# A transformer block on one core: values of two head groups projected at once, the second group's kept in DRAM

## The reference

```python
# 1. token mixer: a state space kernel with 64 poles per channel
K = jnp.einsum('chn,hnl->chl', Cm, jnp.exp(dtA[:, :, None] * jnp.arange(512)))
h = 2 * K.real
# 2. attention on layernorm(h): 16 query heads, 4 key/value heads of width 128, rotary
q = q * cos + _rotate_half(q) * sin
k = k * cos + _rotate_half(k) * sin
k = jnp.repeat(k, 4, axis=1); v = jnp.repeat(v, 4, axis=1)
probs = softmax(q @ k.T / sqrt(128) + bias)        # causal
h = h + (probs @ v) @ w_o
# 3. gated feed-forward on layernorm(h): the best of 8 gates picks a rank 8 update
h = h + _L0_ffn_ref(_layernorm(h, axis=-1), ...)
```

## Time and profile before

| | us |
|---|---|
| median of three runs | 817.11 (816.69 to 817.26) |
| profiled execution | 815.06, span of its records 813.3 |
| TensorE busy | 747.9 |
| VectorE, ScalarE, GpSimd busy | 569.0, 455.8, 445.2 |
| a step of group 1 | 19.94 |
| a loop step of group 3 | 24.5 to 24.7 |
| from the scores of the last step to the end | 43 |

### The profile page before, as it was taken

The page is one execution under the profiler, slowest core; times in us unless marked ns, Lnnn a source line. Parts: engine busy times, 40 slices in busy tenths (PEclk is TensorE's granted clock), DMA queues, the critical chain, the costliest instruction groups (busy, mean ns, idle before and its releaser), DMA issues.

```text
span 813.3 us, 19702 instructions
## 1 busy us (share of the span) xinstructions
PE 747.9 (92%) x6970; PEld 678.4 (83%) x6970; DVE 569.0 (70%) x1600; ACT 455.8 (56%) x1250; POOL 445.2 (55%) x660
## 2 busy tenths in 40 slices
PE   0366778999999999999999999999999999999997
PEld 0166667899999999999999999999999999988974
DVE  7999758787766666665566655665665777788777
ACT  6734426666665656555575665555756556455442
POOL 1497836754444747444456474444656655665632
PEclk9999999999999999999999999999999999999999
DMA  9023360100010102000001020000010000000002
GB/s 213 1 60 69 81 233 27 39 1 0 0 40 2 53 1 79 0 0 0 0 1 52 2 79 0 0 0 0 14 40 1 2 1 27 26 26 0 26 1 104
DMA packets 30503, 26.47 MB, mean 33 GB/s; under 512 B 22446, under 2 KB 22830, under 8 KB 30198
## 3 DMA queue, kind: packets, MB, share of 16 engines
q1 hardware_dynamic: 30310, 25.77, 11.2%
q10 hardware_dynamic: 144, 0.07, 0.0%
HBM read 17.44 MB, written 8.39 MB: 32 GB/s over the span
## 4 chain that ended last, share of the span: by engine, by line
PE 77%; DVE 8%; POOL 7%; ACT 4%; issue 3%; DMA 1%; DVEq 0%; SPq 0%; POOLq 0%; ACTq 0%
PE bank_quad L1324 17%; PE bank_quad L1326 16%; PE bank_quad L1325 16%; PE bank_pair L1326 4%; PE bank_pair L1324 4%; PE bank_pair L1325 4%; POOL w_lo L433 2%; PE bank_quad L1336 2%; PE bank_quad L1425 2%; PE bank L1501 1%; PE bank_pair L1491 1%; PE bank L1505 1%; PE bank_pair L1501 1%; DVE bank_pair L974 1%; POOL kq_lo L511 1%
## 5 line engine op out<-in xcount | busy, mean ns | idle before, releaser
L1324 PE MATMUL bank_quad<-xt_hi,w_hi 128*128 (+1 forms) x768 | 217.0, 282 | 1.4 <-POOL w_lo L433 0.8
L1326 PE MATMUL bank_quad<-xt_lo,w_hi 128*128 (+1 forms) x768 | 214.7, 280 | 0.0
L1325 PE MATMUL bank_quad<-xt_hi,w_lo 128*128 (+1 forms) x768 | 214.5, 279 | 0.0
L1062 DVE TENSOR_TENSOR kq<-bank_quad,cst 128x512 f32<-128x512 f32 (+1 forms) x96 | 57.8, 602 | 134.8 <-ACT swap L725 101.2
L506 POOL TENSOR_TENSOR swap<-swap,cst 128x512 f32<-128x512 f32 (+1 forms) x96 | 105.7, 1103 | 82.2 <-ACT swap L725 77.2
L1324 PEld LDWEIGHTS bank_quad<-xt_hi,w_hi 128*128 128x128 f32 x768 | 144.5, 188 | 3.9 <-issue 1.7
L1326 PEld LDWEIGHTS bank_quad<-xt_lo,w_hi 128*128 128x128 f32 x768 | 144.5, 188 | 0.0
L1325 PEld LDWEIGHTS bank_quad<-xt_hi,w_lo 128*128 128x128 f32 x768 | 144.4, 188 | 0.0
L357 POOL TENSOR_TENSOR spare<-cst 1x1 f32<-1x1 f32 x85 | 17.5, 206 | 204.3 <-DVE rinv L1206 140.0
L768 ACT ACTIVATE sm<-sm,mx 128x128 f32<-128x128 f32 (+1 forms) x256 | 113.5, 445 | 20.6 <-DVE mx L1194 20.6
L724 ACT ACTIVATE swap<-bank_quad 64x512 f32<-64x512 f32 (+1 forms) x96 | 50.2, 523 | 118.6 <-PE bank_quad L1326 115.7
(11 more groups left out here) (313 smaller groups left out, 1861.7 us busy)
## 6 DMA issues: line engine op xcount, KB each, us to landing
mixed<-st SPq DMA_DIRECT2D x32, 128.0 KB, 2.0
out<-x SPq DMA_DIRECT2D x16, 256.0 KB, 2.0
raw<-in_w_qkv SPq DMA_DIRECT2D x8, 384.0 KB, 3.7
raw<-in_w_o SPq DMA_DIRECT2D x10, 256.0 KB, 2.6
x<-mixed SPq DMA_DIRECT2D x2, 1280.0 KB, 10.4
norm_mem<-in_w_qkv SPq DMA_DIRECT2D x6, 384.0 KB, 3.7
x<-mixed SPq DMA_DIRECT2D x3, 512.0 KB, 4.6
norm_mem<-in_w_o SPq DMA_DIRECT2D x6, 256.0 KB, 2.8
```

Of the source, the lines that this page charges most:

```text
L1062: v.tensor_tensor(view(kq), src, table(cosT), ALU.mult).then_inc(kq_cos, 1)
L1324: mmul(dst, lh, rh, start=start and k == 0, stop=False, skip_group_check=True)
L1325: mmul(dst, ll, rh, start=False, stop=False, skip_group_check=True)
L1326: last = mmul(dst, lh, rl, start=False, stop=stop and k == n - 1, skip_group_check=True)
```

## The change

`w_qkv` blocks of even groups get a seventh column block, the value columns of the next, odd group. In the steps that project for an even group, `project_v` makes the values of both groups: the tokens are the stationary operand and the two value blocks (128 columns each, apart in memory) the moving one, so values come out with tokens on the partitions, both groups' side by side in bank 0. The own group's are used at once. The next group's are copied to `v_next` by ScalarE (`keep_next_v`) and stored to DRAM, one DMA a batch. In odd groups no value is projected; one DMA a batch loads it back. `vt` and the transposes of values are gone. `project_v` stands behind the queries, ahead of the transposes of probabilities. Keys now go to bank 7 in even groups and bank 0 in odd ones, and attention to banks 1 and 2. Weights of the feed-forward and `mt` share memory with the `raw` slots and are loaded in the last group. TensorE's loops over b in groups 0 and 2 are written out.

```diff
-WC = HD + HD + QH * HD
+WC = HD + 2 * HD + QH * HD
...
-def steps(engine, body):
+def steps(engine, body, unrolled=()):
 
     for g in range(NG):
-        for lo, hi in RUNS[g]:
+        for lo, hi in [(b, b + 1) for b in range(RUNS[g][0][0], NB)] if g in unrolled else RUNS[g]:
...
+def w_width(g):
+
+    return WC if g % 2 == 0 else WC - HD
+
+
+def key_bank(g, b):
+
+    return 7 if g % 2 == 0 or (isinstance(b, int) and b == 0) else 0
+
+
+def step_after(g, b, at):
+
+    return (g, b + 1) if at < NB - 1 else (g + 1, 0)
+
...
-        fw = sb("fw", [P, KC, FC])
-        dw = sb("dw", [MC, D])
+        fw = raw[:, 0, 0:KC * FC].rearrange("p (k f) -> p k f", k=KC)
+        mt = raw[0:MC, 0, KC * FC:KC * FC + S]
+        dw = raw[0:MC, 1, 0:D]
...
+        def v_of(half):
+
+            return banks[0].rearrange("p (t c) -> p t c", t=TT)[:, :, half * HD:(half + 1) * HD]
...
-                src = w_qkv[g, k] if k < KC else w_o[g, k - KC]
-                sp.dma_start(raw_chunk(n), src).then_inc(raw_in[raw_slot(n)], 16)
+                if k < KC:
+                    sp.dma_start(raw_chunk(n)[:, 0:WC - HD], w_qkv[g, k]).then_inc(raw_in[raw_slot(n)], 16)
+                    if g % 2 == 0:
+                        sp.dma_start(raw_chunk(n)[:, WC - HD:WC], w_qkv[g + 1, k, :, HD:2 * HD]).then_inc(
+                            raw_in[raw_slot(n)], 16)
+                else:
+                    sp.dma_start(raw_chunk(n), w_o[g, k - KC]).then_inc(raw_in[raw_slot(n)], 16)
...
+            def store_v(g, b):
+                sp.wait_ge(v_next_done, (g // 2) * NB + b + 1)
+                sp.dma_start(v_dram[b], later).then_inc(v_stored, 16)
+
+            def load_v(g, b):
+                sp.wait_ge(v_stored, 16 * (g // 2 + 1) * NB)
+                if b:
+                    sp.wait_ge(v_lo, g * NB + b)
+                sp.dma_start(later, v_dram[b]).then_inc(v_loaded, 16)
+
+            def load_ffn():
+                wait_split(sp, NCK * NG - QH)
+                sp.dma_start(fw[:], w_gate).then_inc(ffn_in, 16)
+                wait_split(sp, NCK * NG - QH + 1)
+                sp.dma_start(dw[:], w_upd).then_inc(ffn_in, 16)
...
+            store_v(0, 0)
+            load_raws(KC + 2, NCK)
+            store_v(0, 1)
+            load_raws(NCK, NCK + 2)
+            store_vs(0, 2, NB - 2)
+            load_raws(NCK + 2, NCK + KC)
+            store_vs(0, NB - 2, NB)
+            load_v(1, 0)
+            load_raws(NCK + KC, 2 * NCK)
+            load_vs(1, 1, 3)
+            load_raws(2 * NCK, 2 * NCK + KC)
+            load_vs(1, 3, NB)
+            load_raws(2 * NCK + KC, 3 * NCK)
+            store_vs(2, 0, 2)
+            load_raws(3 * NCK, 3 * NCK + KC)
+            store_vs(2, 2, NB)
+            load_v(3, 0)
+            load_raws(3 * NCK + KC, 4 * NCK)
+            load_vs(3, 1, 3)
+            load_ffn()
+            load_vs(3, 3, NB)
...
+                    hi, lo = wk[:, k, 0:w_width(n // NCK)], wl[:, k, 0:w_width(n // NCK)]
...
+                    src = banks[keys][:, 0:S] if j == 0 else banks[j][:].rearrange("p (h s) -> p h s", h=2)
                     nc.scalar.activation(view(sw)[0:64], src[64:128], ACT.Copy)
-                    last = nc.scalar.activation(view(sw)[64:128], src[0:64], ACT.Copy)
-                    if j == 0:
-                        last = nc.scalar.activation(vt[:], banks[0][:, S:2 * S], ACT.Copy)
-                    last.then_inc(swapped, 1)
+                    nc.scalar.activation(view(sw)[64:128], src[0:64], ACT.Copy).then_inc(swapped, 1)
...
+            def round_v(g, b):
+                if g % 2 == 0:
+                    act.wait_ge(v_ready, b + ((g // 2) * NB + 1))
+                    nc.scalar.activation(vh[:], v_of(0), ACT.Copy).then_inc(v_hi, 1)
+                else:
+                    act.wait_ge(v_loaded, b * 16 + 16 * ((g // 2) * NB + 1))
+                    nc.scalar.activation(vh[:], v_next[:], ACT.Copy).then_inc(v_hi, 1)
+
+            def keep_next_v(g, b):
+
+                if g % 2 == 0:
+                    act.wait_ge(v_ready, b + ((g // 2) * NB + 1))
+                    if g or not isinstance(b, int) or b:
+                        act.wait_ge(v_stored, b * 16 + 16 * (g // 2) * NB)
+                    if g and isinstance(b, int) and b == 0:
+                        act.wait_ge(v_lo, g * NB)
+                    nc.scalar.activation(v_next[:], v_of(1), ACT.Copy).then_inc(v_next_done, 1)
...
                 i = b + 8 * g
+                after = step_after(g, b, at)
                 exponents(i)
-                swap(i + 1, (0,))
+                swap(i + 1, (0,), key_bank(*after))
                 if needs_xt(g, at):
                     xt1(b + 2)
                 if needs_ffn(g, at):
@@ -802,8 +893,9 @@
                     act.wait_ge(o_ready, 8 * g * 2)
                     for k in range(KC, NCK):
                         split_hi(g * NCK + k)
+                keep_next_v(*after)
                 round_attn(i)
-                round_v(i + 1)
+                round_v(*after)
                 if needs_ffn(g, at):
...
             round_probs(0)
+            swap(1, (2,))
             round_kq(1, (1,))
-            swap(1, (2,))
...
-                v.tensor_tensor(vl[:].rearrange("p t d -> p (t d)"), banks[bank][:, 0:S],
-                                vh[:].rearrange("p t d -> p (t d)").bitcast(F32), ALU.subtract).then_inc(v_lo, 1)
+                v.tensor_tensor(vl[:], v_of(0) if g % 2 == 0 else v_next[:], vh[:].bitcast(F32),
+                                ALU.subtract).then_inc(v_lo, 1)
...
-            def w_parts(b, c):
-                cols = slice(c * HD, (c + 1) * HD)
+            def w_parts(b, first):
+                cols = slice(first, first + HD)
                 return [(wk[:, k, cols], wl[:, k, cols], xt_h[:, b, k, :], xt_l[:, b, k, :]) for k in range(KC)]
 
-            def project_kv(b):
-                split_product(banks[0][:, 0:S], w_parts(b, 0))
-                split_product(banks[0][:, S:2 * S], w_parts(b, 1)).then_inc(proj, 1)
-
-            def project_q(b, j):
+            def project_k(g, b):
+                split_product(banks[key_bank(g, b)][:, 0:S], w_parts(b, 0)).then_inc(proj, 1)
+
+            def project_q(g, b, j):
                 for h in range(2):
-                    last = split_product(banks[1 + j][:, h * S:(h + 1) * S], w_parts(b, 2 + 2 * j + h))
+                    last = split_product(banks[1 + j][:, h * S:(h + 1) * S], w_parts(b, (2 + 2 * j + h) * HD))
                 last.then_inc(proj, 1)
 
-            def project(s, b, after_kv, before_last):
-
+            def project_v(g, b):
+
+                pair = lambda w, k: w[:, k, HD:].rearrange("p (n c) -> p n c", c=HD)[:, 0:6:5, :]
+                for t in range(TT):
+                    rows = slice(t * P, (t + 1) * P)
+                    last = split_product(banks[0][:, t * 2 * HD:(t + 1) * 2 * HD].rearrange("p (n c) -> p n c", c=HD),
+                                         [(xt_h[:, b, k, rows], xt_l[:, b, k, rows], pair(wk, k), pair(wl, k))
+                                          for k in range(KC)])
+                last.then_inc(v_ready, 1)
+
+            def project(s, g, b, after_k, before_last):
+
+                if g % 2:
+                    pe.wait_ge(v_next_done, (g // 2 + 1) * NB)
+                project_k(g, b)
+                after_k()
                 pe.wait_ge(ot_lo, s * 2 - 3)
-                project_kv(b)
-                after_kv()
+                project_q(g, b, 0)
                 pe.wait_ge(ot_lo, s * 2 - 2)
-                project_q(b, 0)
-                pe.wait_ge(v_lo, s)
                 before_last()
-                project_q(b, 1)
-
-            def turn_v(bank):
-                for t in range(TT):
-                    last = nc.tensor.transpose(banks[bank][:, t * P:(t + 1) * P], vt[:, t * P:(t + 1) * P], ident)
-                last.then_inc(vt_ready, 1)
-
-            def transpose_v(s):
-                pe.wait_ge(swapped, s * 3 + 3)
-                pe.wait_ge(kq_cos, s * 3 + 3)
-                turn_v(2)
+                project_q(g, b, 1)
+                if g % 2 == 0:
+                    pe.wait_ge(v_lo, s)
+                    pe.wait_ge(v_next_done, b + (g // 2) * NB)
+                    project_v(g, b)
...
+                        if at == 2:
+                            pe.wait_ge(ffn_in, 32)
...
                     wait_split(pe, (g + 1) * NCK + KC - 1)
-                project(i + 1, (b + 1) if at < NB - 1 else 0, after_kv, before_last)
+                project(i + 1, *step_after(g, b, at), after_k, before_last)
                 pe.wait_ge(pt_lo, i * 3)
+                pe.wait_ge(swapped, i * 3 + 4)
+                pe.wait_ge(kq_cos, i * 3 + 4)
...
                 out_product(i - 1)
-                transpose_v(i + 1)
                 pe.wait_ge(swapped, i * 3 + 6)
...
-            project_q(1, 0)
+            project_q(0, 1, 0)
             pe.wait_ge(xn_ready, 3)
```

(59 more changed lines are left out.)

78 lines of the change are left out of this document (38 added, 40 removed).

## The result

The changed kernel took 818.68 us (median of 14 executions, 817.25 to 819.73) against 817.19 for the kernel before (14, 814.92 to 818.34): ratio 1.0021, 95% interval 1.0014 to 1.0029. The forecast was 818.8. Its profiled execution took 819.69 (span 817.9), the one before 815.06, so the two traces to be compared lie 4.6 us apart, and the medians 1.5: the traced execution of the kernel before is 2 us shorter than its median, that of the changed one 1 us longer. The ratio lies at the edge of the 0.2% that the prediction took as the border between slower and same.

A forecast was written before the change was run, and what follows sets the result against it. The prediction took TensorE, busy 92% of the span, as the bound, with VectorE's chain tied to it in the last group. Terms -6.7 + 8.0 + 1.0 + 0.4 - 1.0 = +1.7 us on the 817.11 median gave 818.8 us, range 812 to 823.

The forecast's parts named there:

- 32 pairs of transposes: One pair of value transposes removed from each of the 32 steps, 0.21 us a pair: -6.7 us.
- pitch of value products: Value products keep their number and width, nearest known spacing 0.1178 us: taken as 0.
- last group, five light steps: TensorE's saving there is not gained, as it must wait for VectorE's masks or the tokens: +8.0 us together.
- tokens' transposes, four steps: First group: keys alone end before the masks whose banks the transposes reuse, 0.24 us a step: +1.0 us.
- exchange of weights: Steps (g, 6): GpSimd's wider blocks for group 2 cost +1.2 us, the other two exchanges -0.4 each: +0.4.
- start: Up to step (0, 1): added value products cover part of TensorE's waits; bounds -2.5 to +2.5, taken as -1.0 us.
- clock: Third rival: clock falls at each of the last group's five waits, at least 7 us, 825.8 us; chance 0.03.
- The step on which the forecast rested: Last group: VectorE's chain, 14.3 us from projection's end to last mask, keeps its length, tied to TensorE's within 0.13 us.
- Rival 1: Light steps pay everywhere because VectorE's chain isn't rigid; the 8.0 falls away: 810.8 us; chance 0.22, whole or in part.
- Light and heavy steps: Now 19.94 us: group 1's light steps would take 18.3 us, group 2's heavy ones 21.1.
- rival 2: The start gets slower, value products delaying batch 1; decided from a net loss of 1 us; 822.3 us; chance 0.15.
- Costed at nothing: ScalarE's copies, DRAM stores and loads of values, GpSimd's wider first blocks and unrolled loops: 0 us.

The follow-up runs named there:

- before_again: The kernel before, unchanged, run once more for a second trace: 816.41 us.
- no_turn: The kernel before without the transposes of values in all but the first two steps (attention's result left out): 811.39 us, 0.9934.
- fill: The changed kernel with twelve unread key products more ahead of update_product in each of the last group's steps 3 to 6: 815.82 us, 0.9986.
- hoist_half: The changed kernel with half the first query pair projected ahead of update_product and the tokens' transposes, in last-group and some first-group steps: 806.55 us, 0.9875.
- fill_again: fill run once more, unchanged: 816.60 us, 0.9994 of the kernel before.
- fill_v_late: fill with the value products of (0, 1) behind the first batch's transposes of probabilities, two time-filling products dropped: 813.89 us, 0.9968.
- fill6: fill with six dummy products a step instead of twelve: 816.13 us, 0.9993.
- v_late: The changed kernel with the value products of (0, 1) behind the first batch's transposes of probabilities, two time-filling products dropped: 817.73 us, 1.0010.
- before_hoist: The kernel before with only the new order of hoist_half: 816.46 us, 0.9992.
- hoist_full: hoist_half with the whole first query pair moved ahead, and the gate product between the halves of the second pair: 807.38 us, 0.9869.

## Why the prediction was right

The sum first, on the traced executions, taken from the starts of all 32 scores. Without the two falls the changed kernel is 1.4 us longer; I had 1.7. Against before_again it is 0.1 longer, so the sum of a single pair of traces is good to some 1.3 us.

| Term | Predicted | Measured | From |
|---|---|---|---|
| 32 pairs of transposes | -6.7 | -8.0 | no_turn: 0.24 to 0.27 a pair |
| pitch of value products | 0 | -1.4 | 2.73 us for 24: 0.1138 each |
| last group, five light steps | +8.0 | +8.4 | steps as long as before; lost 5 x (1.41 + 0.25), and 0.1 |
| tokens' transposes, four steps | +1.0 | +1.4 | steps 22.23, not 20.81 |
| exchange of weights | +0.4 | +0.3 | +1.5, -0.8, -0.4 (against before_again +1.2, -0.8, -0.8) |
| start | -1.0 | +0.3 | +1.5 and -1.2, see below |
| tail | 0 | +0.4 | last scores to the end: 43.6, not 43.2 |
| clock | 0 | +3.2 | two falls of 1.6 |

- **The chain that isn't idle decides.** The step on which the forecast rested held: the loop steps without a fall and (3, 2) kept their length, VectorE's chain its 14.3 us, and TensorE got the waits of 1.4 us put down to the masks. fill, hoist_half and no_turn show it from three sides. Rival 1 is out for the change as it is. It was right only in that some 10 us lay there, for another order.
- **Light and heavy steps** came close to the forecast: 18.26 (18.3), 20.98 to 21.00 (21.1), 22.23 in the first group. There the four steps cost 0.1 more each than the 0.24 that I had, if measured from a heavy step of group 2.
- **The clock was an error.** I gave falls 0.03 because one wait of 1.79 us had shown none in one execution. In three traces of the changed last group, five of twelve waits of 1.4 us were followed by one; in fill, fill_again and fill_v_late, without the waits, none of twelve steps had one. By the medians the falls are worth 2 to 3 us. The Trainium skill, "TensorE: Matmul & The Clock Gate", "What's actually happening", has TensorE at its lower clock when it has been idle; it spoke against the change, and the traces agree in direction, at some waits and not at all of them.
- **What met.** On the traces the sum without falls came out at 1.4 for my 1.7 because its terms erred both ways: transposes and value products gave 2.7 us more than I had, the other terms took 2.4 more, the start 1.3 of them. The two falls come on top, so the traced difference is 4.6. On the medians, from which my 818.8 is made, the changed kernel without falls is 0.5 to 1.1 us below the kernel before (fill, fill_again, fill6), 2 to 3 us under my +1.7, and the falls brought it up to +1.5. I had added the 2.05 between trace and median without asking what is in it; the kernel before loses time at a lower clock in some executions as well.
- **The start:** rival 2's mechanism was real, its size is not settled. Twelve more products ahead of the first scores show no cost (125.62 against 125.79), which the table books as a gain of 1.2; but the first scores start at 124.87 to 127.19 over the traces, so one pair can't show it. In (0, 0) and (0, 1) 1.5 us are lost, by the excess of the two steps over what the steady terms give. Whether that makes the net loss of 1 us from which rival 2 decides stays open. Its mechanism is what v_late removes: (0, 0) is 2.3 shorter. The waits there are the 1.9 us above, which was 1.79 before, and a new one of 1.7 us in (0, 1), where keys alone no longer cover the masks ahead of the tokens' transposes; hoist_half brings that to 0.23.
- **Costed at nothing:** the loads land in 1.9 to 2.1 us each, and no wait of ScalarE is put down to one. Looped and unrolled light steps both last 18.26. The tail's 0.4 I did not look into.
- **The spread.** The prediction's "814.5 to 822" is not the plain sum of the ends of its terms, which is 813 to 827.

So the sum was right in its structure, VectorE's chain above all, and the closeness to 818.8 is partly luck: on the medians a sum that was 2 to 3 us too high met falls of the clock that it had at nothing.

## What to carry to other kernels

Before you take work off a saturated engine, find for each kind of step the second chain and its length from the event that starts it: where it is tied, the saving becomes a wait. The order of work that made no difference clear of the noise while both chains were full (before_hoist) then becomes the lever: work that waits for nobody goes ahead of the wait (12 us here, some 3 of them falls of the clock). And price the waits that a change makes on TensorE beyond their length: a trace without a fall shows one execution, so look at several.

## What the runs showed of the hardware

- Behind waits of 1.4 us in the last group the granted clock fell to 0.50 five times in twelve, for about 3 us, at 1.6 us a fall, not always in the same steps. Behind 0.6 us (fill6) it did not in four, nor behind the 1.6 to 1.7 us in (3, 2) and (0, 1) in any trace. Behind 1.8 to 1.9 at the start it fell in two traces (hoist_full, before_hoist) and not in nine others. What decides between a fall and none isn't shown.
- Products of 256 columns at a granted clock of 1.00 started at one of two distances, 0.1133 to 0.1138 us or some 0.1178. In most steps the value products (tokens stationary, the moving operand in two pieces of 128 columns) had the shorter one and those with the weights stationary the longer. The form alone doesn't decide it. The weights' products had 0.1133 in (1, 7) and (2, 7) of the first trace of the kernel before and 0.1177 in the second. The value products had 0.1178 in (1, 7) of hoist_half, and in v_late, where they stand behind transposes; its second and last there:

```profile
136.10 0.28 PE L1419 MATMUL bank_quad<-w_hi,xt_lo 128*128 128x256 f32 x1
...
138.69 0.28 PE L1420 MATMUL bank_quad<-w_lo,xt_hi 128*128 128x256 f32 x1
```

That is 22 starts in 2.59 us. I have no cause for it.
